# The first slot table of a mixture-of-experts stage: counted over 12 batches, built one iteration sooner, and slot 0 put in another order on TensorE

## What is computed

```python
x = x + attn(layernorm(x), W_qk, W_v, slope)      # causal, one head, alibi bias
x = x + xattn(layernorm(x), ctx, ctx, mask, ...)  # 16 heads of 16, over a context of 256 rows
x = x + ffn(layernorm(x), w_gate, w_gate_up, w_down)

def ffn(x, w_gate, w_gate_up, w_down):            # E = 8 experts, F = 1024, top 2 of 8
    probs = softmax(x @ w_gate)
    topk_vals, topk_idx = top_k(probs, 2)
    gate = masked(topk) / sum(topk_vals)          # zero for experts that a token didn't choose
    g, u = split(einsum('bsd,edh->ebsh', x, w_gate_up))
    return einsum('bse,ebsd->bsd', gate, einsum('ebsf,efd->ebsd', silu(g) * u, w_down))
```

## Time and profile before

| what | value |
|---|---|
| median of 3 runs | 1108.24 us |
| the runs | 1108.24, 1104.51, 1108.52 us |
| span of the profiled execution | 1101.4 us |
| TensorE busy, mean granted clock | 95% of the span, 0.990 |
| VectorE, ScalarE, GpSimd busy | 60%, 59%, 47% |

### The profile page before, as it was taken

One profiled execution on the slowest core, in us unless ns is written; L12 is line 12 of the kernel. 1 busy time (PEld: TensorE's weight loads), 2 busy tenths in 40 slices (PEclk: granted clock), 3 DMA queues, 4 the chain that ended last, 5 costly groups with the idle time before them and its releaser, 6 DMA issues.

```text
span 1101.4 us, 36849 instructions
## 1 busy us (share of the span) xinstructions
PE 1042.1 (95%) x12742; PEld 884.4 (80%) x12742; DVE 666.3 (60%) x2153; ACT 654.7 (59%) x1439; POOL 522.1 (47%) x563
## 2 busy tenths in 40 slices
PE   4789999999999999889999999999999999999996
PEld 2457677777777776548899999999999999999996
DVE  5667788888888887854564444444444444444443
ACT  6588889888888888664443443444344344344332
POOL 4756677777777777423352332324323323323322
PEclk9899999999999999999999999999999999999999
DMA  5754666666666663386222451294221221238211
GB/s 181 238 187 161 170 174 176 172 181 181 179 182 181 183 183 108 107 297 232 45 37 36 143 152 29 46 393 113 33 34 29 33 33 29 37 100 297 42 29 20
DMA packets 91943, 142.76 MB, mean 130 GB/s; under 512 B 21232, under 2 KB 69808, under 8 KB 88560
## 3 DMA queue, kind: packets, MB, share of 16 engines
q1 hardware_dynamic: 76062, 122.96, 35.8%
q0 software_dynamic: 15808, 19.09, 10.7%
q10 hardware_dynamic: 18, 0.01, 0.0%
HBM read 268.13 MB, written 43.47 MB: 283 GB/s over the span
## 4 chain that ended last, share of the span: by engine, by line
PE 83%; DVE 6%; SPq 3%; ACT 3%; issue 2%; DMA 2%; POOL 1%; DVEq 0%; ACTq 0%; POOLq 0%
PE front L2307 17%; PE t_ring L2307 17%; PE s_ring L2325 8%; PE pv L2325 8%; PE pv L2022 5%; PE s_ring L1989 5%; PE t_ring L2007 5%; PE front L1864 4%; PE s_ring L1851 2%; PE front L1873 2%; PE front L1922 2%; PE tail L1873 2%; DVE nmax L1284 2%; PE tail L1851 1%; PE front L1851 1%
## 5 line engine op out<-in xcount | busy, mean ns | idle before, releaser
L787 POOL DMA_INDIRECT out<-y_sb,place_i x71 | 112.3, 1582 | 316.9 <-DVE y_sb L1761 121.9
L2307 PE MATMUL front<-rows_hi,wgu_sb 128*128 128x128 f16 x2272 | 213.5, 219 | 1.6 <-DVE rows_lo L1736 1.6
L2307 PE MATMUL t_ring<-rows_hi,wgu_sb 128*128 128x128 f16 x2272 | 214.6, 220 | 0.0
L1284 DVE TENSOR_REDUCE nmax<-s_ring 128x2 f32<-128x512 f32 x256 | 167.5, 682 | 53.7 <-PE s_ring L1989 52.5
L2307 PE MATMUL t_ring<-rows_lo,wgu_sb 128*128 128x128 f16 x1136 | 198.6, 220 | 0.0
L2307 PE MATMUL front<-rows_lo,wgu_sb 128*128 128x128 f16 x1136 | 197.6, 219 | 0.0
L2307 PEld LDWEIGHTS front<-rows_hi,wgu_sb 128*128 128x128 f16 x2272 | 180.5, 98 | 4.1 <-DVE rows_lo L1736 2.1
L2307 PEld LDWEIGHTS t_ring<-rows_hi,wgu_sb 128*128 128x128 f16 x2272 | 181.3, 98 | 1.6
L954 ACT ACTIVATE probs_t<-t_ring,mask_bias 128x512 f32<-128x512 f32 x256 | 167.1, 705 | 22.4 <-PE t_ring L2007 20.3
L1144 ACT ACTIVATE silu_g<-t_ring 128x256 f32<-128x256 f32 x142 | 54.6, 385 | 167.8 <-PE t_ring L2307 167.8
L1792 DVE SCALAR_TENSOR_TENSOR act_t<-t_ring,silu_g 128x256 f32<-128x256 f32 x142 | 60.3, 425 | 152.2 <-ACT silu_g L1144 152.2
(11 more groups left out here) (248 smaller groups left out, 2100.6 us busy)
## 6 DMA issues: line engine op xcount, KB each, us to landing
wgu_sb<-gu_split SPq DMA_DIRECT2D x71, 2048.0 KB
wd_sb<-down_split SPq DMA_DIRECT2D x71, 1024.0 KB
w_piece<-in_w_gu SPq DMA_DIRECT2D x32, 512.0 KB, 6.4
gu_split<-w_halves SPq DMA_DIRECT2D x32, 512.0 KB, 3.8
w_piece<-in_w_down SPq DMA_DIRECT2D x16, 512.0 KB, 7.6
down_split<-w_halves SPq DMA_DIRECT2D x16, 512.0 KB, 5.2
x_in<-in_x SPq DMA_DIRECT2D x16, 256.0 KB
ctx_in<-in_ctx_t_in SPq DMA_DIRECT2D x16, 256.0 KB
```

Of the source, the lines that this page charges most:

```text
L787: nc.gpsimd.indirect_dma_start(out=out, out_offset=bass.IndirectOffsetOnAxis(ap=place_i[:, j:j + 1], axis=0), in_=y_sb[:, j], in_offset=No ...
L1284: nc.vector.tensor_reduce(nmax[:, n // HJ, :, n % HJ], s_ring[n % 2][:].rearrange("p (r k) -> p r k", r=2), AX.X, ALU.max, negate=True).th ...
L2307: o = nc.tensor.matmul(gu_ring[f][:, part * SLOT:(part + 1) * SLOT], wgu_sb[j][:, w, at:at + P], r[:, j % 2, c], start=(i == 0), stop=(i = ...
```

## The change

- `EARLY_TOKENS` and `EARLY_STRIDE` go from 13 to 12. SyncE and GpSimd wait for one batch less of scatters and of stored rows before the first slots.
- VectorE builds the early table in iteration 13 of its loop, between the division of the attention output and the first two maxima. The functions are moved ahead of `iteration` as they are.
- The four `slot_rows` take the table's place at the start of iteration 14.
- TensorE: what is left of slot 0 is written out in `first_slot`; `t_rank` of batch 14 goes behind both `gate_up` groups, and `down` and `t_queries` behind it. VectorE's `t_place` of batch 14 goes from part f = 2 to f = 3 of slot 0.

```diff
-EARLY_TOKENS = 13
-EARLY_STRIDE = 13
+EARLY_TOKENS = 12
+EARLY_STRIDE = 12
+TABLE_BATCH = EARLY_TOKENS + 1
...
@@ vector: iteration(b, p, h, c, t, s, f, n)
                 if n:
                     f_stats1(b + 3, 1 - p, h + 1 + p)
                     f_aggr1(b + 3)
+                if isinstance(b, int) and b == TABLE_BATCH:
+                    for part in range(3):
+                        early_table(part)
                 if s:
                     h_max(b + 1, 0, 2)
...
@@ vector: last_tail(s, f)
-                if s == 0 and f == 2:
+                if s == 0 and f == 3:
                     t_place(B - 2, 0)
...
@@ vector: last_maxima()
                 t_norm(b - 1, tail, s_ring[1])
-                early_table(0)
-                early_table(1)
-                early_table(2)
+                for j in range(STREAMS):
+                    slot_rows(j, j, 0)
                 h_max(b + 1, 0, 4)
                 t_stream(b - 1)
                 h_max(b + 1, 4, 6)
                 t_norm3(b - 1, 1, b // 2 - 1)
                 h_max(b + 1, 6, 12)
                 t_logits(b - 1)
-                for j in range(STREAMS):
-                    slot_rows(j, j, 0)
                 h_max(b + 1, 12, 16)
...
@@ tensor: last_tail(s, f)
-                if s == 0 and f == 1:
-                    t_rank(B - 2)
-                if s == 0 and f == 3:
-                    t_queries(B - 1, 1, pv)
...
+            def first_slot():
+                rows_transposed(1, 1, 0)
+                gate_up(0, 0, 2)
+                gate_up(0, 0, 3)
+                t_rank(B - 2)
+                down(0, 0, 0, 0)
+                t_queries(B - 1, 1, pv)
+                down(0, 0, 0, 1)
+
             last_attention()
-            for s in range(2 * STREAMS):
+            first_slot()
+            for s in range(1, 2 * STREAMS):
                 slot(s, s % STREAMS, s // STREAMS, True)
```

More of the change, by code:

```diff
@@ L1466, in t_place, with then, count_rows, slots_of @@
                 t_pos_i(c, p)
+            step = [2]
+            def then(ins):
+                step[0] += 1
+                ins.then_inc(slot_step, 1)
+                vec.wait_ge(slot_step, step[0])
+            def count_rows(tokens):
+                vec.wait_ge(rank_sb, tokens)
+                then(nc.vector.tensor_tensor(count[:], next_row[0:1], region0[0:1], ALU.subtract))
+            def slots_of(added):
+                if added:
+                    then(nc.vector.tensor_scalar(count[:], count[:], float(added), None, ALU.add))
+                then(nc.vector.tensor_copy(count_i[:], count[:]))
+                then(nc.vector.tensor_scalar(slots_i[:], count_i[:], SLOT.bit_length() - 1, None,
+                                             ALU.arith_shift_right))
+                then(nc.vector.tensor_copy(slots_f[:], slots_i[:]))
@@ new lines, in ends_of, with jumps @@
+            def ends_of(slots, n0, n):
+                then(nc.vector.tensor_tensor_scan(slot_end[:], one_e[:], slots[:], 0.0, ALU.mult, ALU.add))
+                then(nc.vector.tensor_tensor(past[:, 0:n], slot_end[:].unsqueeze(1).to_broadcast([1, n, E]),
+                                             slot_id[:, n0:n0 + n].unsqueeze(2).to_broadcast([1, n, E]), ALU.is_le))
+            def jumps(n):
+                then(nc.vector.tensor_scalar(jump[:], jump_use[:], float(SLOT), float(REGION), ALU.mult, ALU.add))
+                then(nc.vector.tensor_tensor(past_jump[:, 0:n], past[:, 0:n], jump[:].unsqueeze(1).to_broadcast([1, n, E]),
+                                             ALU.mult))
@@ new lines, in experts, with slot_firsts @@
+            def experts(n0, n):
+                at = slice(n0, n0 + n)
+                then(nc.vector.tensor_reduce(slot_e[:, at], past[:, 0:n], AX.X, ALU.add))
+                then(nc.vector.tensor_scalar(slot_ec[:, at], slot_e[:, at], float(E - 1), None, ALU.min))
+                then(nc.vector.tensor_copy(slot_tab[:, 1, at], slot_ec[:, at]))
+            def slot_firsts(n0, n):
+                at = slice(n0, n0 + n)
+                then(nc.vector.tensor_reduce(slot_r[:, at], past_jump[:, 0:n], AX.X, ALU.add))
+                then(nc.vector.scalar_tensor_tensor(slot_r1[:, at], slot_order[:, at], float(SLOT), slot_r[:, at],
+                                                    ALU.mult, ALU.add))
@@ L1646, in _ @@
             attention_loop(vec, first_fronts, iteration)
[L1649 to L1710, removed]
```

19 lines of the change are left out of this document (added).

## The result

| | before | changed |
|---|---|---|
| median (lowest to highest) of 6 runs each, us | 1107.07 (1104.01 to 1108.83) | 1112.42 (1111.59 to 1115.36) |
| ratio, 95% interval | 1 | 1.0059 [1.0043, 1.0076] |
| span of the profiled execution, us | 1101.4 | 1110.1 |
| its own device time, us | not listed | 1111.87 |

The changed kernel is slower by 5.4 us between the medians and by 0.0059 x 1107 = 6.5 us by the ratio. In the thirteen profiled executions whose own time is listed (all but that of before) it is 1.7 to 1.9 us above the span. So the profile of before stands for a time of about 1103.2 us, the low end of its runs (1102 to 1109 us on all chips), and the 8.7 us between the two spans overstate the loss by some 2 to 3 us.

The account below looks back on a forecast made before the run. TensorE is almost never idle in the slots, so only slot 1's start can move. Terms +0.8 + 3.2 - 0.9 = +3.1 us gave span 1104.5 us; adding 6.8 us gave 1111.3 us, range 1105.5 to 1115.

Parts of the forecast that it names:

- Rival 2: Waits cost their upper ends: slow landings behind stores, low TensorE clock, iteration 13 losing 1.8 us; +6.9 us, 1115 us; chance 0.13.
- Iteration 13: Table built before VectorE's first maxima: GpSimd blocks some instructions, first maximum 1.5 us late, 0.8 us lost (0 to 1.8).
- Iteration 14: At its start, four `slot_rows` wait for entries' DMAs, delaying the maxima 3.2 us; net +3.2 us (1.3 to 6).
- the four go out at 459.4: SyncE's queue in iteration 14: four entry loads issued at 459.4 to 462.85 us, fourth index there at 464.75 us.
- The credits of 0.45 and 0.7 us: Iteration 14: 0.45 us back at the old `slot_rows` place, some 0.7 because late VectorE finds its scores ready.
- the clock's 1.1 us: Iteration 14: TensorE, idle over 3 us, then runs at half speed, adding 1.1 us.
- Slot 0: TensorE's wait for `chosen` gives way to waits for `act_lo` and `next_row`; slot 1 starts 0.9 us earlier (2.8 gain to 0.3 loss).
- The rival that saw 2.8 us in it: Iteration 14 costs 1 us or less, slot 0 gains 2.8; sum -1.5 to -2 us, 1106.5 us; chance 0.22.
- The table from 12 batches and the weights: In the slots, streams change expert elsewhere, with 11 new weight loads instead of 9; worth 0.
- Rival 4: In the slots, new loads of weights make TensorE wait; chance 0.02.

## Why the prediction held, and where its sum failed

The forecast of 1111.3 us (range 1105.5 to 1115) stands against 1112.42 us. That nearness is partly luck: the working gave +3.1 us, and measured were 5.4 to 6.5, while the median that it was added to (1108.24 us, of three runs) lay 1.2 us above that of six, 1107.07. The 6.8 us from the span to the median did no harm, since adding them is the same as starting from the median, but they are no constant: an execution's own time stands 1.8 us above its span, and the rest says that the profiled one was fast. The two traces give 2.1 + 5.3 + 0 = 7.4 us for the three terms, more than the medians, since that fast execution is one of the two. The ratio lies at the 0.5% mark, 1.0059 on one chip and 1.0050 on the other, so the 0.84 for "within 0.5%" was too sure and 0.12 for slower too little. Rival 2's sizes were nearly the case, its 1.8 us of iteration 13 and most of its 6 us; its cause, slow landings, was not: the load that ended the wait landed within 2.0 us.

1. **Iteration 13, +0.8 (bounds 0 to 1.8); measured +2.1.** The mechanism held, GpSimd shutting VectorE out. The size did not: I had counted on one full hit and one or two of 0.2 to 0.5 us, there were two full and two of 0.59 us, and one of the two full hits fell on a CAST, an instruction with one input, that I had not named among the exposed. The Trainium skill, "SBUF — State Buffer", "Who interferes with whom", names the shared port pair as an exclusive lock. The rows agree, and so does the run with GpSimd held back (0.16 instead of 1.08 us for `count_i`). Of the 2.4 us delay only 0.3 was made up; I had expected 0.7, having read the small waits behind the hole as slack. So 2.1 us lies above the stated bound of 1.8.
2. **Iteration 14, +3.2 (bounds 1.3 to 6); measured +5.3.** What waits, for whom and what queues behind came as the prediction had it, and taking the place back brought most of the loss back. The step that went wrong is "the four go out at 459.4", 3.4 us after `o_n`; the first went out 4.6 us after it, in both profiles of the changed kernel. SyncE loses 1 us on a slow issue, in the first at `q_hi` (2.22 us for two instead of 1.24, as taken from the profile of before), in the second at `out` (1.52 instead of 0.51). I had taken issue times from an execution without one; of 14 profiles 12 have one, of 0.4 to 1.1 us. From its last store to the first load it took 1.31 us instead of 1.06. The first index was there 3.5 us after the issue of its load, later than the 1.7 to 1.9 us of the estimate, but the fourth, which ends the wait, after 2.0 us, nearly as estimated. The credits of 0.45 and 0.7 us and the clock's 1.1 us were to cancel nearly (-0.05); measured was +0.8, a stage that takes 18.16 to 20.40 us in the kernels whose first table is built as before.
3. **Slot 0, -0.9 (bounds -2.8 to +0.3); measured 0.** Both waits came as foreseen, 0.81 and 1.57 us against 0.8 and 2; the error is the clock behind them. At full clock, in one profile, the order brings 1.5 us. The rival that saw 2.8 us in it needed `next_row` earlier; with `t_rank` and `t_place` moved the other order gives 2.9 us in the stage.
4. **The table from 12 batches and the weights, 0:** right within 0.6 us. Rival 4 fell.

What the sum lacked altogether is that with the whole table in iteration 13 the first scores of iteration 14 come later behind the DMAs of batch 15's queries, for a reason that stays open. It hides in the changed kernel, whose first maximum waits for the entries anyway, and shows once the rows are back.

## What to carry to other kernels

An instruction that waits for a DMA costs what stands behind it on its engine: put it after work that is ready, and where a hole is to be filled, count the other engine's work in it, for this chain of small instructions met each of GpSimd's. A wait of TensorE that is cut into two can pay again in the clock; look for the order that removes it. Take issue times from several executions of a queue, not from one.

## What the hardware did that I had not expected

- A CAST of 8 elements with one SBUF input took 1.08 us beside a GpSimd subtraction, just as a two-input instruction did, and one of 16 elements 0.59 us; left alone they take 0.16 us.
- TensorE's clock behind a wait does not follow from that wait alone: after 1.71 us it stayed at 1.00, after 2.14, 2.61 and 4.12 us it went down to 0.50 (1.2 GHz) for 2 us or more, after one of 0.69 us it was 0.63 and 0.52 in one profile and after one of 0.88 us 1.00 in another, and after the same 1.57 us it was 1.00 here and 0.72 there.
- SyncE takes 0.6 us to issue a DMA of 128 KB, but in 12 of 14 profiles one of the seven DMAs from `k_lo` to `out` takes 0.4 to 1.1 us more, and the whole queue behind it is late by that.
